# Attention outputs from rotated query operands of 512 tokens, edge scores of four steps at once, and a later place for a wait of the gathers

## The reference

```python
# edges, sorted by their target row
e = leaky_relu(a_src . Wh[row] + a_dst . Wh[col]);  alpha = softmax of e over each row's edges
h_new = segment_sum(Wh[col] * alpha, row) + Wh
# mixing attention, 8 heads of 32
q, k = normalised heads;  v1 = [1, v] / N
kv_mod = einsum('ni,nj,ne->ije', k, k, v1);  kv = einsum('nd,ne->de', k, v1)
y = 0.5 * einsum('ni,nj,ije->ne', q, q, kv_mod) + c1 * einsum('nd,de->ne', q, kv) + c2 * sum(v1)
y = y[:, 1:] / y[:, :1];  out = concat_heads(y) @ Wproj.T + bproj
```

## Time and profile before

| | |
|---|---|
| plain runs, median of 3 | 3498.43 us (3497.71 to 3507.61) |
| profiled execution, span | 4552.4 us |
| PE / DVE / ACT / POOL busy, share of that span | 68% / 61% / 43% / 47% |
| DMA moved | 452.9 MB |
| largest groups | L884 gathers on POOL 1504 us, L2046 edge sums on PE 1053 us, L1565 weighing on DVE 534 us, L1582 features on DVE 478 us |

### The profile page before, as it was taken

One profiled execution on the slowest core, in us unless ns is written; L12 is line 12 of the kernel. 1 busy time (PEld: TensorE's weight loads), 2 busy tenths in 40 slices (PEclk: granted clock), 3 DMA queues, 4 the chain that ended last, 5 costly groups with the idle time before them and its releaser, 6 DMA issues.

```text
span 4552.4 us, 80191 instructions
## 1 busy us (share of the span) xinstructions
PE 3118.0 (68%) x17657; PEld 2176.0 (48%) x17657; DVE 2760.2 (61%) x6376; ACT 1951.9 (43%) x5742; POOL 2159.7 (47%) x2438
## 2 busy tenths in 40 slices
PE   4888266666666666667777777777776444777895
PEld 2333133333333333456555555555555333666785
DVE  8999866666666666656555555565555465434322
ACT  4777133333333333344444444444444222544674
POOL 5877455455555555544444444444444532123123
PEclk8888677777887877788888888888888776988998
DMA  2222244343434434433333333333333333334344
GB/s 67 99 96 89 89 103 103 106 103 101 110 100 104 121 99 105 110 89 90 84 92 81 87 89 83 83 87 85 84 88 83 94 112 130 105 109 150 96 136 134
DMA packets 326431, 452.92 MB, mean 99 GB/s; under 512 B 79020, under 2 KB 261482, under 8 KB 326052
## 3 DMA queue, kind: packets, MB, share of 16 engines
q0 software_dynamic: 85552, 236.37, 19.0%
q1 hardware_dynamic: 217896, 194.32, 14.9%
q10 hardware_dynamic: 22860, 20.83, 1.6%
HBM read 366.49 MB, written 84.82 MB: 99 GB/s over the span
## 4 chain that ended last, share of the span: by engine, by line
PE 27%; DVE 21%; issue 20%; another core or an unknown queue 15%; DVEq 7%; ACT 5%; POOL 3%; ACTq 1%; DMA 1%; SPq 1%; POOLq 0%
PE bank L2046 8%; PE bank L2230 4%; PE bank L2242 4%; DVE room L1582 3%; PE bank L2080 3%; DVE room L1374 2%; DVEq L1541 2%; PE bank L2091 2%; DVE room L1373 2%; DVE room L1565 2%; DVE room L1535 1%; DVE room L1555 1%; PE bank L2055 1%; ACT room L1175 1%
## 5 line engine op out<-in xcount | busy, mean ns | idle before, releaser
L884 POOL DMA_INDIRECT room<-table,room x1564 | 1504.4, 962 | 1594.4 <-DVE room L1565 1127.9
L2046 PE MATMUL bank<-room 128*128 128x260 f32 x3520 | 1053.1, 449 | 472.4 <-DVE room L1565 291.2
L2046 PEld LDWEIGHTS bank<-room 128*128 128x128 f32 x3520 | 752.3, 225 | 634.4 <-issue 510.2
L1565 DVE TENSOR_TENSOR room<-room,bank 128x1024 f32<-128x1024 f32 x440 | 534.3, 1214 | 71.3 <-issue 41.1
L1582 DVE TENSOR_TENSOR room<-bank,room 128x1024 f32<-128x1024 f32 x392 | 477.5, 1218 | 162.6 <-remote 88.9
L1175 ACT ACTIVATE room<-bank 128x512 f32<-128x512 f32 (+1 forms) x588 | 252.4, 487 | 393.0 <-remote 306.0
L1555 DVE TENSOR_REDUCE room<-bank 128x32 f32<-128x128 f32 x440 | 125.2, 285 | 426.9 <-remote 263.8
L1107 ACT ACTIVATE bank<-room 128x16 f32<-128x16 f32 x440 | 80.8, 184 | 671.8 <-DVE room L1559 432.9
L1100 ACT ACTIVATE spare<-away,ones 128x512 bf16<-128x512 bf16 x440 | 317.6, 722 | 57.3 <-ACT away L1097 7.6
L2080 PE MATMUL bank<-ident,room 128*128 128x128 f32 x1764 | 298.8, 325 | 22.3 <-issue 11.1
L1115 ACT ACTIVATE bank<-room 128x96 f32<-128x96 f32 x392 | 96.4, 246 | 506.5 <-DVE room L1585 331.5
(11 more groups left out here) (321 smaller groups left out, 5010.7 us busy)
## 6 DMA issues: line engine op xcount, KB each, us to landing
spare<-rows_dram SPq DMA_DIRECT2D x440, 128.0 KB
room<-table,room POOLq DMA_INDIRECT x1564
kv_dram<-room SPq DMA_DIRECT2D x49, 324.0 KB, 2.2
room<-kv_dram SPq DMA_DIRECT2D x196, 81.0 KB
y_dram<-planes SPq DMA_DIRECT2D x119, 128.0 KB
room<-xs_dram ACTq DMA_DIRECT2D x110, 128.0 KB
q_dram<-room SPq DMA_DIRECT2D x49, 192.0 KB, 1.9
room<-q_dram SPq DMA_DIRECT2D x196, 48.0 KB
```

The source lines that it names most:

```text
L884: pool.indirect_dma_start(G[:, k.slot, u, :], None, table, bass.IndirectOffsetOnAxis(ap=ixbuf[:, k.slot, u:u + 1].bitcast(I32), axis=0)).t ...
L1565: dve.tensor_tensor(Gw[:, h, :, 0:C].rearrange("p u (h d) -> p u h d", h=GH), G[:, bass.ds(slot, 1), :, 0:C].rearrange("p a u (h d) -> p ( ...
L2046: ins = pe.matmul(pbank[1 + h][:, 0:TW], OH[:, s, u, :], Gw[:, h, u, :], start=(u == 0), stop=(u == U - 1))
```

## The change

Query operands are kept transposed. In stage 1, two tiles behind, PE turns a tile's padded q in three transposes (`turn_q`), ACT copies them (`copy_qt`) and SP stores them as `qt_dram`, 384 rows (8 heads x 48) by tokens, in the place of `q_dram`. In the query stage a group is 512 tokens (13 groups, the last of 128), and takes four laps, two heads a lap. SP loads, for each head, `rot_a` (the 32 values four times, on 128 partitions) and `rot_b` (for each of four starting shifts d, four more shifts of 4c), so that one DVE product of [128, 2, 512] a step gives two of the four 128-row chunks of features, already with features on partitions. PE multiplies them as they are, `kvm` as the stationary operand and 512 columns moving; the transposes, their ACT copies and ACT's copy of q to PSUM are gone. The tail is a separate product of 512 columns once a lap. Turning back, dividing and projecting are done for one tile of 128 tokens a lap, five laps behind. The features have four buffers instead of two, also in the key stage.

The target scores of a whole lap are made in one burst: ACT makes OHT two laps ahead, PE runs four steps' `row_scores` behind the fourth step into one bank, DVE takes all four with one reduction (`take_scores`) in the third step. The one-hots read the index row from PSUM in all laps. `report` comes two groups behind, after the first indirect DMA. W2 is loaded after the last product of the query stage. Rows of targets are loaded two laps ahead.

```diff
         def load_q(q, s):  ... (removed)
+        def load_rot(gq, h):
+            r, w = h % 2, width(gq)
+            n = 8 * gq + h
+            if not isinstance(n, int) or n >= 2:
+                sp.wait_ge(qf_done, 2 * n - 2)
+            tok = bass.ds(gq * QW, w)
+            for d in range(4):
+                sp.dma_start(rot_a[d * MD:(d + 1) * MD, r, 0:w], qt_dram[h * XD:h * XD + MD, tok]).then_inc(unit_loaded[r], 16)
+                rows = bass.AP(qt_dram.tensor, qt_dram.offset + (h * XD + d) * NP, [[NP, MD], [4 * NP, FCH], [1, NP]])
+                sp.dma_start(rot_b[d * MD:(d + 1) * MD, r, :, 0:w], rows[:, :, tok]).then_inc(unit_loaded[r], 16)
+        def load_tail(gq, p):
+            if not isinstance(n, int) or n >= 1:
+                sp.wait_ge(qtail_done, n)
+            if not isinstance(n, int) or n >= 2:
+                sp.wait_ge(y_step, 4 * n - 7)
...
+        def q_group(gq):
+            for l in range(QG):
+                n = 4 * gq + l
+                for s in range(4):
+                    load_row(At(n + (LAPS_K + 2), s, 4))
+                    if s == 0:
+                        load_tail(gq, l)
+                    if s % 2 == 0:
+                        load_rot(gq, 2 * l + s // 2)
+                    if s == 1 and (not isinstance(n, int) or n >= 7):
+                        store_mix(n - 7)
+        sp.wait_ge(y_step, 16 * NQG)
+        for e in range(XE):
+            sp.dma_start(w2[:, e, :, :], t["W2"][e].rearrange("(c p) n -> p c n", p=P)).then_inc(s_w4e, 16)
...
-                if u == 2 and k.after(1):
-                    report(k + -1)
+                if u == 0 and k.after(2):
+                    report(k + -2)
...
+        def take_scores(lap):
+            dve.wait_ge(s_made, lap + 1)
+            if not isinstance(lap, int) or lap > 0:
+                dve.wait_ge(z_done, 4 * lap)
+            dve.tensor_reduce(row_sum[:, :].rearrange("p (u n) -> p u n", n=2 * GH),
+                              score_ps[:, :].rearrange("p (u j n) -> p u n j", j=4, n=2 * GH), AX.X, ALU.add).then_inc(scores_taken, 1)
...
-            o.then(dve.tensor_reduce(ps, parts, AX.X, ALU.add))
...
+        def q_features(gq, l, s):
+            if s == 0:
+                dve.wait_ge(unit_loaded[2], 16 * ((KL - 1) * PAIRS + T_LOADS * (4 * gq + l + 1)))
+                x = tail_x[:, l % 2, 0:w]
+                dve.tensor_tensor(x, x, tail_y[:, 0:w], ALU.mult).then_inc(qtail_done, 1)
+            dve.wait_ge(unit_loaded[r], 16 * ((KL if r == 0 else KL - 1) * PAIRS + R_LOADS * (4 * gq + l + 1)))
...
+                dve.wait_ge(y_step, n - 3)
+            c = 2 * (s % 2)
+            dve.tensor_tensor(feat[:, s, :, 0:w], rot_a[:, r, 0:w].unsqueeze(1).to_broadcast([P, 2, w]),
+                              rot_b[:, r, c:c + 2, 0:w], ALU.mult).then_inc(qf_done, 1)
...
+        def y_part(gq, l, s):
+            out = y_bank(l)[:, 0:w]
+            if s == 0:
+                pe.matmul(out[0:HEAD2 + V1, :], kv_tail[:, l, :], tail_x[:, l % 2, 0:w], start=True, stop=False, skip_group_check=True)
+            pe.wait_ge(qf_done, n + 1)
+            for j in range(2):
+                c = 2 * (s % 2) + j
+                ins = pe.matmul(out[p0:p0 + V1, :], kvm[:, h, c, :], feat[:, s, j, 0:w],
+                                start=False, stop=(c == FCH - 1), skip_group_check=True)
+            ins.then_inc(y_step, 1)
...
                 sum_rows(k)
-                if (k + 2).inside(STEPS):
-                    row_scores(k + 2)
                 if extra is not None:
                     extra(s)
+                if s == 3 and (k + 8).inside(STEPS):
+                    row_scores(i + 2)
```

451 lines of the change are left out of this document (253 added, 198 removed).

## The result

| | before | after |
|---|---|---|
| plain runs, median | 3500.51 us (3497.71 to 3507.61, 4 runs) | 3580.78 us (3577.39 to 3583.62, 4 runs) |
| ratio after / before | | 1.0228, 95% interval 1.0214 to 1.0243 |
| profiled execution, span | 4552.4 us | 3579.6 us |
| instructions | 80,191 | 68,996 |

The changed kernel is 2.3% slower. The forecast of 3450 us had the wrong sign.

A forecast was written before the change was run, and what follows sets the result against it. It took DVE with POOL 12 us behind to bound the key stage, DVE and PE the query stage, POOL the plain one. 3498.4 - 5 (key stage) - 52 (query and plain) + 9 (W2) = 3450 us, range 3370 to 3575.

The forecast's parts named there:

- start of the edge steps: Ahead of the key stage: POOL starts about 4 us later, for added fills and masks.
- key stage, by itself: Key stage: DVE saves 0.44 us a step, at most 92 us, but POOL's limit leaves 8; with the announcement, gain 5.
- query and plain stages without DMA's limit, W2 included: Query and plain stages: 1133 us against 1185, gain 52; moving W2's loads costs 9.
- the extra loads: Query stage: a lap moves 5.4 MB instead of 2.7, 17 to 20.8 us of DMA; cost taken: nothing.
- DMA bounds the query lap: Rival, query stage: rot loads against gathers on DMA engines; at 235 GB/s the lap is 23.0 us, total 3580; chance 0.19.
- POOL is 12 us behind: Key stage: POOL's groups end at 1523, DVE's own time at 1535, so only 12 us lie between them.
- Landing: POOL's announcement of a group: 2.6 us later when POOL is the limit, once, not per step.
- Query lap: Query stage: PE 18.8, DVE 18.4, POOL 18.1 us a lap; taken as 20.3, bounds 18.8 and 21.3.
- POOL held by DVE's products: Rival, query stage: each POOL group loses one 1.22 us product, lap 22.5 us, total 3556; chance 0.06.
- W2: After the last head product: eight loads of 4.2 MB go ahead of lap 106's rows; cost 9 us (0 to 18).
- Stage one: Projections and sort: transposes and copies hide under DVE's sort, 0 us (bounds 0 to 8); fills and masks start POOL 4 us later.
- Signs named beforehand: Profile after: key step 4.3 us, query lap near 20.3, DMA share above 0.5; wrong if laps exceed 21.3 or products await loads.

The follow-up runs named there:

- c_before: The kernel before, unedited, run again on the same chip as c_after: 3507.4 us.
- c_after: The changed kernel, unedited, run again on the same chip as the kernel before: 3579.8 us, ratio to before 1.0227.
- e14: Three idle memsets a group added on POOL, to the changed kernel with rotated operands loaded over 128 partitions: 3442.5 us.
- e15: An idle 128-column reduction a step added on DVE, to the changed kernel with rotated operands loaded over 128 partitions: 3562.4 us.
- e5: Changed kernel with rotated operands loaded over all 128 partitions, rows interleaved so a load's first dimension is 32: 3408.9 us, ratio to before 0.9744.
- e18: The kernel before with only the landing report moved, two groups behind after the first gather: 3505.2 us, ratio 1.0005.
- e17: e5 with the loads of W2 moved behind SP's last row loads: 3397.95 us, ratio to before 0.9697.
- e16: e5 with each load of rotated operands cut into two of 64 partitions, lower and upper half in turn: 3452.1 us.
- e2: Changed kernel with rotated operands loaded for only 128 of 512 tokens from the second group on; on a chip with stops: 4232.6 us.
- e3: Changed kernel with W2's loads moved behind SP's last row loads, on a chip with stops: 4194.9 us, ratio to before 0.9355.

## Why the prediction was wrong, step by step

The sum was 3498.4 - 5 - 52 + 9. Its model of before was 50 us high as a whole: the experts' 830 us held stops, as guessed (762.0 in c_before), while the key stage (994 against 1011.0) and the plain one (143 against 156.4) were priced too low. On one chip c_before's profiled execution and c_after's differ by 79.6 us, and the steps are now separable:

| step | forecast, us | measured, us | from |
|---|---|---|---|
| start of the edge steps | +4 | +9.3 | c_before, c_after |
| key stage, by itself | -9 (with the start: -5) | -68.8 | c_before, c_after; e14, e15 |
| query and plain stages without DMA's limit, W2 included | -52 + 9 = -43 | -44.7 | e5 |
| the extra loads | 0 | +177.5 | c_after against e5 |
| last stage | 0 | +6.5 | c_before, c_after; cause open |

*The extra loads* ("Cost taken: nothing") is the step that failed and the one that turned the sign. The bytes were right: 5.4 MB a lap over 23.8 us is 227 GB/s, and the trace says 228. The time for them was wrong. It was scaled from rows whose transfers are spread over all partitions, where a busy share of 33% at 86 GB/s makes 260. For e5's loads that scaling is safe (271 GB/s at 0.88 makes 308, between the prediction's 260 and 315). For loads to 32 partitions it is not: 228 at 1.01. The rival "DMA bounds the query lap" had place and mechanism, decided at 253 GB/s, and gave 23.0 us and 3580; measured were 23.8 and 3581. That it meets the total is luck: its loads cost 130 us and not 177.5, and the key stage gave back 60 us more than its sum held. It priced a rate "10% under" without a reason; the reason was in the diff, in the destination's `d * MD:(d + 1) * MD`, 32 partitions. Against it stood the cover of 14 us between a buffer's release and its use. That cover hides a delay of one load, but no shortage of rate, which adds up from lap to lap. The 358 GB/s of HBM, which the prediction cites, was no bound here: no query stage moved more than 271, and at the same bytes from HBM the partitions written and their order made it 228 to 271.

*Key stage.* DVE's step was priced right: 0.44 us forecast, 4.79 to 4.35 measured, 92 us at most. The step that failed is "POOL is 12 us behind". It let the stage consume 196 groups, the number of attention units, and so POOL end at 1523. The stage has 208 steps and 391 groups go into 440 steps, 185 groups, the number that the earlier trace rows gave as 741/4. With it POOL ends at 521.9 + 185 x 5.11 = 1467, not 12 but 86 us before the 1552.8 at which the stage ends in c_before. The changed stage ends at 1493.3; by then POOL has begun 188 groups, 5.14 us apart on average, from 528.1 on. The model put the end at 1535. Mechanism right (POOL becomes the limit: e14), size 60 us short, for a miscount.

*Landing.* 2.6 us were forecast as its cost where POOL is the limit; e18 says 0 on before, where it is not. In the changed kernel it is not parted from the rest.

*Query lap.* Forecast 20.3 us from PE, DVE and POOL within 0.7 of one another; e5's is 20.07, before's 20.97 (21.26 forecast). The PE terms stand: edge sums 2.0, head products 1.9 (1.8 forecast), the tail 1.0 (0.9). Some 19 us of e5's stage are what four long steps, of 8.2 to 11.0 us where 4.6 are usual, take too much: the 64th, 96th, 128th and 160th, where the loop of eight laps jumps back; before, with a loop of one lap, has none. The trace has 112 packets on an instruction queue in this stage and 5 in before's. The Trainium skill, "Runtime: NRT & Kernel Launch", section "Instruction fetch mechanics", says that a taken branch out of the loaded window makes the engine wait for a fetch; the places agree. A loop of four laps was not tried.

*POOL held by DVE's products.* Gathers take 1057 ns in e5's query stage (736.81 us for 697) and 954 in its key stage; before 979. So something lengthens them by 0.08 to 0.1 us, in the direction of that rival; but the DMA engines are busier as well (0.87 against 0.51 in before), and no run parts the two. A group takes 5.5 us (median) and not 6.33, and the lap of 22.5 did not come: e5 has 20.07 with the same products.

*W2.* Forecast 9, e17 says 11.

*Stage one.* The fills were sized about right (4,096 + 512 + 1,024 columns and the masks): the first gather is at 526.4 in after and 528.1 in c_after, where c_before has 522.9, so 3.5 and 5.2 us later against 4. What was left out is that the first score now needs the one-hots and matmuls of four steps: DVE waits 7.26 us where it waited 1.66.

*What is left over.* 6.5 us of the last stage, in every kernel with the changed query path (765 to 770 against 761 to 762). It isn't W2 (e17 has 767.8). 4.3 us of it lie in one place, ahead of POOL's reduction over partitions behind the last step; here c_before, then c_after:

```profile
2752.66 0.39 POOL L922 PARTITION_ALL_REDUCE mxs<-dmax  x1 [5.91 <-issue]
2831.76 0.39 POOL L996 PARTITION_ALL_REDUCE mxs<-dmax  x1 [10.19 <-issue]
```

What POOL does in these gaps the trace doesn't say, so the cause stays open.

*Signs named beforehand.* Key step 4.3 on DVE with POOL without idle time: came. No L2080 and one stop of ACT (22.4 us): came. DMA share above 0.5: came, and at 1.01 it should have been named as the sign of failure. A lap near 20.3 with PE nearly gapless: did not come, PE is busy for 958 of the 1157 us. Of the signs of being wrong all three came: query laps of 23.8 us, products that wait 149.1 us for their loads, and gathers of 1057 ns.

## What to carry to other kernels

Before adding traffic, ask of each new load which partitions it writes and what the first dimension on both sides is, and price it by packets of that form, not by a GB/s of other transfers. Once the DMA share of a stage reaches 1, as here, a cover of 14 us between release and use doesn't hide the loads; a wider destination (e5) or an order that alternates between the halves (e16) helped. Fewer bytes should too, but e2 ran among stops and doesn't show it. Where several engines run within a few per cent, count the work of each stage by what that stage consumes (groups by steps), because the gain of shortening one engine is the distance to the next.

## What the runs showed of the hardware

- A packet of 2048 bytes takes 84 ns where loads write 128 partitions, 109 where loads of 64 alternate between the halves, 140 where 64 of one half follow each other, 153 to 32 partitions; the last two with all DMA engines busy at 240 and 228 GB/s.
- SP issues four loads of 256 KB whose first dimension is 4 in 9.33 us, with 3.7 packets under way at once; with the same packets and a first dimension of 32 in 2.72 us, with 8.7 at once.
- The same program takes 3500 us on one chip and 4500 or 4568 on two others, with about one stop a lap (11 us for a step of 4.8 in before's key stage). There e3 is 6.5% faster than before, while c_after, the same but for W2's 11 us, is 2.3% slower where there are no stops.
- Three memsets of 8 columns add only 0.10 us to a POOL group of 5.10, and all of it shows in a stage that POOL sets.
